# Self attention of a decoder layer: K and Q projected once a batch on 128 rows and spread to row groups through DRAM; the first cross transposes placed in the self attention's ring of banks

## What is computed

```
x = _layernorm(x + self_attention(x))
x = _layernorm(x + cross_attention(ctx_1024, x, mask))
x = _layernorm(x + experts(x))

# self attention, x: [8, 256, 128]
q, k, v = x @ Wq.T, x @ Wk.T, x @ Wv.T         # split into 16 heads of 8
scores = einsum('bhtc,bhkc->bhtk', q, k) * 8 ** -0.5, causal
out = softmax(scores) @ v, heads joined, @ Wo.T
```

## Time and profile before

| | us |
|---|---|
| median of 3 runs | 1153.52 (1153.27 to 1154.64) |
| the profiled execution | 1154.32 |
| its span, from first to last instruction | 1152.5 |
| PE busy | 1104.0 (96%) |
| DVE busy | 879.1 (76%) |
| ACT busy | 735.5 (64%) |
| POOL busy | 539.6 (47%) |
| mean granted clock of TensorE | 0.996 |

### The profile page before, as it was taken

How to read it: one execution, slowest core, us unless ns; L and a number is a source line. 1 busy time by engine, 2 the same in 40 slices (tenths; PEclk the granted TensorE clock), 3 DMA queues, 4 the chain that set the end, 5 groups by cost and what they waited for, 6 DMA issues and landing times. The chain is left out here.

```text
span 1152.5 us, 27526 instructions
## 1 busy us (share of the span) xinstructions
PE 1104.0 (96%) x8781; PEld 946.9 (82%) x8781; DVE 879.1 (76%) x2786; ACT 735.5 (64%) x1754; POOL 539.6 (47%) x892
## 2 busy tenths in 40 slices
PE   6999997999999999999999999999999998999997
PEld 5888875778888887887888888888788887999997
DVE  7999996888878788778787878877878685655554
ACT  6999996667757666666765766666667565322221
POOL 4666665554574355446456445544644432400101
PEclk9999999999999999999999999999999999999999
DMA  2000011000000000000000000000000003000000
GB/s 92 7 7 11 7 44 38 1 11 1 2 1 11 2 1 11 1 1 11 2 1 1 11 2 1 2 1 2 1 2 1 2 1 96 3 10 6 11 6 11
DMA packets 14685, 12.39 MB, mean 11 GB/s; under 512 B 1361, under 2 KB 13649, under 8 KB 14417
## 3 DMA queue, kind: packets, MB, share of 16 engines
q1 hardware_dynamic: 14128, 10.43, 3.0%
q10 hardware_dynamic: 416, 0.20, 0.1%
HBM read 9.57 MB, written 1.05 MB: 9 GB/s over the span
## 5 line engine op out<-in xcount | busy, mean ns | idle before, releaser
L874 POOL TENSOR_TENSOR xk_parts<-k_raw,xk_parts 64x768 fp32r<-64x768 f32 x128 | 236.1, 1845 | 312.7 <-DVE xk_parts L992 310.0
L1016 DVE CUSTOM_DVE_ANT_0 xmasked<-ps,bar 128x768 f32<-128x768 f32 x256 | 244.3, 954 | 4.2 <-issue 0.6
L1128 PE MATMUL ps<-xk_parts,xq_parts 128*128 128x512 f32 (+1 forms) x1024 | 233.2, 350 | 6.9 <-DVE xq_parts L997 3.4
L929 ACT ACTIVATE xprobs<-xmasked,xlow 128x768 f32<-128x768 f32 x256 | 238.0, 930 | 1.4 <-DVE xlow L1016 1.4
L1134 PE MATMUL ps<-ident,xprobs 128*128 128x128 f32 x1536 | 215.0, 276 | 7.1 <-DVE xlow L1016 6.0
L1128 PEld LDWEIGHTS ps<-xk_parts,xq_parts 128*128 128x128 f32 x1024 | 174.4, 189 | 33.3 <-DVE xq_parts L997 3.8
L1134 PEld LDWEIGHTS ps<-ident,xprobs 128*128 128x128 f32 x1536 | 168.9, 140 | 16.7 <-DVE xlow L1016 10.8
L1145 PE MATMUL ps<-xprobs_t,xvals 128*64 128x256 f32 x1536 | 179.9, 383 | 1.1 <-ACT xprobs_t L935 1.1
L1145 PEld LDWEIGHTS ps<-xprobs_t,xvals 128*64 128x64 f32 x1536 | 104.8, 137 | 57.9 <-issue 10.6
L1021 DVE COPY xprobs_t<-ps 128x768 f32<-128x768 f32 x128 | 121.6, 950 | 3.5 <-PE ps L1134 3.5
L909 ACT ACTIVATE k_raw<-ps 128x768 f32<-128x768 f32 x64 | 52.0, 812 | 105.1 <-PE ps L1102 94.3
(11 more groups left out here) (220 smaller groups left out, 2524.8 us busy)
## 6 DMA issues: line engine op xcount, KB each, us to landing
ctx_in<-in_ctx SPq DMA_DIRECT2D x8, 256.0 KB, 3.3
w_rest<-in_L_ffn_w SPq DMA_DIRECT2D x2, 768.0 KB, 6.4
raw_kv<-in_L_xattn_Wkv SPq DMA_DIRECT2D x1, 1024.0 KB, 5.3
out<-state SPq DMA_DIRECT2D x8, 128.0 KB, 2.0
x_in<-in_x SPq DMA_DIRECT2D x7, 128.0 KB, 2.2
raw_q<-in_L_xattn_Wq SPq DMA_DIRECT2D x1, 512.0 KB, 6.1
wout<-in_L_xattn_Wout SPq DMA_DIRECT2D x1, 512.0 KB, 3.9
keep_all<-in_mask_BxS_bk SPq DMA_DIRECT2D x1, 512.0 KB, 4.7
```

The lines of the kernel that those rows point to most:

```text
L874: pool.tensor_tensor(k_parts[dst, i // 2 % 2, h, :], k_raw[src, :], k_parts[src, i // 2 % 2, h, :].bitcast(F32), ALU.subtract).then_inc(k_ ...
L929: nc.scalar.activation(probs[:, i % 4, :], masked[:, i % 4, :], ACT.Exp, scale=-1.0, bias=low[:, i % 4:i % 4 + 1], accum_out=sums[:, pair ...
L1016: dve.tensor_tensor_reduce(masked[:, i % 4, :], slot(slots.place("S", i), KEYS), bar[:, par, :], 1.0, 3e38, ALU.add, ALU.min, low[:, i % 4 ...
L1128: last = nc.tensor.matmul(slot(s, hi - lo, lo), q_parts[:, pair % 2, h, part, t * P:(t + 1) * P], k_parts[:, pair % 2, h, lo:hi], start=pa ...
```

## The change

**K and Q.** Each batch has one step KQ: six matmuls with the plain 128x128 weights project K and Q for all 16 heads into one bank of 512 columns. ACT rounds the bank once (`flat_hi`), DVE takes the remainder once (`flat_lo`). SP writes both to a buffer in DRAM (256 KB each) and reads them back with six transfers into the row groups of `kq_parts` (`k_parts` and `q_parts` are its halves), each to 32 partitions, four of them of 128 KB and two of 256 KB, 1 MB in all. The reads wait for both writes (`kept`); Q_HEAD and S wait for all six reads (`spread`). `kq_parts` has two halves for batches in turn. The weights are transposed 3 times instead of 9.

**V** is one step of six matmuls and one copy. **x_in** has three buffers instead of two, and SP's list has LOAD(1), then SPREAD(0), SPREAD(1), LOAD(2), SPREAD(2), LOAD(3) and so on, all behind `first_contexts`.

```diff
@@ decoder_layer
+        m.scratch = nc.dram_tensor("flat", [2, 2, P, 2, S], F32, kind="Internal").ap()
-                a.gpsimd(pool, {last: steps(emit, "N1", 5, 0, 1) + steps(emit, "N2", 5, 9, 1),
-                                B: steps(emit, "Y", 1, 9, 1)})
+                a.gpsimd(pool, {B - 2: steps(emit, "N1", 5, 0, 1) + steps(emit, "N2", 5, 9, 1),
+                                last: steps(emit, "Y", 1, 15, 1)})
...
-                a.vector(dve, {B - 2: steps(emit, "STATS", KT, 0, 2),
-                               last: steps(emit, "NORM1", 2, 4, 1) + steps(emit, "NORMED", KT, 13, 0.5),
-                               B: steps(emit, "BAR", 1, 3, 1) + steps(emit, "Y", 1, 7, 1)})
+                a.vector(dve, {B - 3: steps(emit, "STATS", KT, 4, 2),
+                               B - 2: steps(emit, "NORM1", 2, 5, 1),
+                               last: steps(emit, "NORMED", KT, 2, 0.5) + steps(emit, "Y", 1, 12, 1),
+                               B: steps(emit, "BAR", 1, 3, 1)})
@@ self_attention
     pe_order = Order(B, SH, {
-        "S": (SH, -0.5), "PT": (SH, 4.75), "K": (SG, -3.5), "Q": (SG, -4), "V": (T, -4),
-        "T": (1, -5), "R": (SG, 9.75), "PV": (SG, 9.5), "OUT": (1, 24)})
+        "S": (SH, -0.5), "PT": (SH, 4.75), "KQ": (1, -8.25), "V": (1, -8),
+        "T": (1, -10), "R": (SG, 9.75), "PV": (SG, 9.5), "OUT": (1, 24),
+        "TX": (1, -6.5), "TC": (1, -6.25)}, only=FIRST_CROSS)
     dve_order = Order(B, SH, {
-        "S": (SH, -0.5), "K": (SG, -3.5), "Q": (SG, -4.25), "PT": (SH // 2, 5.5),
-        "XLO": (1, -5.25), "RECIP": (SG, 5.75), "NORM": (SG, 10), "OUT": (1, 23.5),
-        "V": (T, -4.5)})
+        "S": (SH, -0.5), "KQ": (1, -7.75), "PT": (SH // 2, 5.5),
+        "XLO": (1, -9.25), "RECIP": (SG, 5.75), "NORM": (SG, 10), "OUT": (1, 23.5),
+        "V": (1, -7.25)})
     act_order = Order(B, SH, {
-        "EXP": (SH, 3), "PT": (SH // 2, 6.75), "K": (SG, -1.75), "Q": (SG, -3), "R": (SG, 11.25),
-        "T": (1, -3.5)})
+        "EXP": (SH, 3), "PT": (SH // 2, 6.75), "R": (SG, 11.25), "KQ": (1, -6), "T": (1, -8),
+        "TX": (1, -4), "TC": (1, -3.75)}, only=FIRST_CROSS)
...
+        def emit(kind, b, par, i):
+            if kind == "LOAD" and b > 0:
+                wait(sp, added, b - 2)
+                wait(sp, loaded_x, 16 * b)
+                sp.dma_start(x_in[:, b % 3, :, :], x_rows[b]).then_inc(loaded_x, 16)
+            if kind == "SPREAD":
+                wait(sp, spread, 96 * b)
+                for n, (flat, done) in enumerate(((flat_hi, flat_hi_done), (flat_lo, flat_ready))):
+                    sp.wait_ge(done, b + 1)
+                    sp.dma_start(m.scratch[par, n], flat[:, :, :].bitcast(F32)).then_inc(kept, 16)
+                wait(sp, full["S"], (b - 1) * SH)
+                sp.wait_ge(kept, 32 * (b + 1))
+                for r, to, part in ((0, slice(0, 2), 0), (1, slice(0, 1), 1), (1, slice(1, 2), 0),
+                                    (2, slice(0, 1), 0), (2, slice(1, 2), 1), (3, slice(0, 2), 1)):
+                    sp.dma_start(kq_parts[32 * r:32 * r + 32, par, to, :, :].bitcast(F32),
+                                 m.scratch[par, part, :, to, :].rearrange("(g p) n c -> p n g c", g=SG)
+                                 ).then_inc(spread, 16)
+        emit("LOAD", 1, 1, 0)
+        for b in range(B):
+            emit("SPREAD", b, b % 2, 0)
+            if 1 <= b < B - 1:
+                emit("LOAD", b + 1, 0, 0)
...
             if kind == "Q_HEAD":
                 g = i // HG
-                pool.wait_ge(q_ready, b * SG + g + 1)
+                pool.wait_ge(spread, 96 * (b + 1))
...
+            if kind == "KQ":
+                act.wait_ge(full["KQ"], b + 1)
+                wait(act, kept, 32 * b)
+                nc.scalar.activation(flat_hi[:, :, :].rearrange("p n s -> p (n s)"), bank(banks.place("KQ", 0)),
+                                     ACT.Copy).then_inc(flat_hi_done, 1)
...
+            if kind == "KQ":
+                dve.wait_ge(flat_hi_done, b + 1)
+                dve.tensor_tensor(flat_lo[:, :, :].rearrange("p n s -> p (n s)"), bank(banks.place("KQ", 0)),
+                                  flat_hi[:, :, :].rearrange("p n s -> p (n s)").bitcast(F32), ALU.subtract
+                                  ).then_inc(flat_ready, 1)
...
+            if kind == "KQ":
+                for n, w in enumerate((1, 0)):
+                    o, wh, wl = bank(s, S, n * S), w_hi[:, w, :], w_lo[:, w, :]
+                    nc.tensor.matmul(o, wh, xt_hi[:, par, :], start=True, stop=False)
+                    nc.tensor.matmul(o, wh, xt_lo[:, par, :], start=False, stop=False)
+                    last = nc.tensor.matmul(o, wl, xt_hi[:, par, :], start=False, stop=True)
+                last.then_inc(full["KQ"], 1)
...
             if kind == "S":
-                pe.wait_ge(k_ready, b * SG + i // HG + 1)
+                pe.wait_ge(spread, 96 * (b + 1))
                 pe.wait_ge(q_head_ready, b * SH + i + 1)
```

More of the change, by code:

```diff
@@ L46, with __init__ @@
 class Order:
-    def __init__(self, batches, units, starts, beyond=()):
-        self.batches, self.beyond = batches, beyond
+    def __init__(self, batches, units, starts, beyond=(), only=(), without=()):
+        self.batches, self.beyond, self.only, self.without = batches, beyond, only, without
         due = []
@@ L65, in has @@
     def has(self, kind, batch):
-        return 0 <= batch < self.batches + (kind in self.beyond)
+        if kind in self.only:
+            return batch == self.batches
+        return 0 <= batch < self.batches + (kind in self.beyond) and (kind, batch) not in self.without
     def run(self, emit, between=None, done=(), left=()):
@@ L338, in self_attention @@
     xt_lo = sb(mem, "xt_lo", [P, 2, S], F32R)
-    round_kq = sb(mem, "round_kq", [P, 2, S], F32R)
-    k_parts = sb(mem, "k_parts", [P, SG, S], F32R)
-    q_parts = sb(mem, "q_parts", [P, 2, S], F32R)
+    flat_hi, flat_lo = (sb(mem, "flat_" + n, [P, 2, S], F32R) for n in ("hi", "lo"))
+    kq_parts = sb(mem, "kq_parts", [P, 2, 2, SG, S], F32R)
+    k_parts, q_parts = (kq_parts[:, :, n, :, :] for n in range(2))
     q_head = sb(mem, "q_head", [P, 4, S], F32R)
@@ L362, in self_attention @@
     weights = sem("a_weights")
-    full = {k: sem(f"a_{k}_full") for k in ("T", "K", "Q", "V", "S", "PT", "R", "OUT")}
+    full = {k: sem(f"a_{k}_full") for k in ("T", "KQ", "V", "S", "PT", "R", "OUT")}
     xh_done, x_ready = sem("a_xh_done"), sem("a_x_ready")
-    kh_done, k_ready = sem("a_kh_done"), sem("a_k_ready")
-    qh_done, q_ready = sem("a_qh_done"), sem("a_q_ready")
+    flat_hi_done, flat_ready = sem("a_flat_hi_done"), sem("a_flat_ready")
+    kept, spread = sem("a_kept"), sem("a_spread")
     q_head_ready = sem("a_q_head_ready")
@@ L417, in sync @@
         first_contexts()
-        def load(kind, b, par, i):
-            if isinstance(b, int) and b == 0:
-                return
-            wait(sp, added, b - 1)
-            wait(sp, loaded_x, 16 * b)
-            sp.dma_start(x_in[:, par, :, :], x_rows[b]).then_inc(loaded_x, 16)
-        Order(B, SH, {"LOAD": (1, -SH)}).run(load)
+        def emit(kind, b, par, i):
[20 more added lines that the diff above has]
+                emit("LOAD", b + 1, 0, 0)
         sp.dma_start(wout[:, :, :], m.xwout.rearrange("(r p) d -> p r d", p=P)).then_inc(loaded_rest, 16)
@@ L469, in gpsimd, with scalar @@
         pool_order.run(emit, between)
-    def scalar(act, between=None):
+    def scalar(act, cross, between=None):
         act.dma_start(x_in[:, 0, :, :], x_rows[0]).then_inc(loaded_x, 16)
@@ L521, in vector @@
         dve.memset(vals[:, :, :, :, :], 0.0)
-        link(dve.memset(part[:, :], 0.0))
-        for rows, col in ((slice(32, 64), 0), (slice(96, 128), 0), (slice(64, 96), 1), (slice(96, 128), 1)):
-            last = dve.memset(part[rows, col:col + 1], -1.0)
-        link(last)
         dve.wait_ge(consts, 5)
@@ L618, in emit @@
                 for j in range(T):
[L619 removed]
+                    last = nc.tensor.transpose(bank(s, P, j * P), x_in[:, b % 3, j, :], ident[:, :])
                 last.then_inc(full["T"], 1)
[L621 to L622 removed]
+            if kind in ("KQ", "V"):
+                pe.wait_ge(weights, 2)
                 pe.wait_ge(x_ready, b + 1)
[L624 to L629 removed]
@@ L630, in emit @@
-            if kind == "V":
-                wh, wl = wv_hi[:, :], wv_lo[:, :]
-                xh, xl = (a[:, par, i * P:(i + 1) * P] for a in (xt_hi, xt_lo))
-                nc.tensor.matmul(bank(s, D), xh, wh, start=True, stop=False)
-                nc.tensor.matmul(bank(s, D), xh, wl, start=False, stop=False)
-                nc.tensor.matmul(bank(s, D), xl, wh, start=False, stop=True).then_inc(full["V"], 1)
+            if kind == "KQ":
[5 more added lines that the diff above has]
+                last.then_inc(full["KQ"], 1)
@@ new lines, in emit @@
+            if kind == "V":
+                wh, wl = w_hi[:, 2, :], w_lo[:, 2, :]
```

(7 more changed lines are left out.)

119 lines of the change are left out of this document (48 added, 71 removed).

## The result

The changed kernel takes 1207.66 us (median; 1206.47 to 1208.38), beside 1153.47 us for the kernel before: a ratio of 1.0467, 95% interval [1.0448, 1.0485]. It is slower by 54 us, where I had forecast +8.3 and a range up to 1174. The sign is right, the size is far off.

The account below looks back on a forecast made before the run. ACT was taken to set the pace, with a DRAM wait added to its loop. Start +7.7, seven passages +3.8, last batch -2.0 and step to cross attention -1.2 gave +8.3 us: 1162 us forecast, range 1155 to 1170, eight in ten 1147 to 1174.

Parts of the forecast that it names:

- the second loop: From ACT's T over xt_lo, KQ, V and OUT to R(0): stall 2.6 us, floor 21.4 us a batch.
- the step to the cross attention: Passing from self to cross attention: -1.2 us, between 0 and -2, including cross Q(0) starting 0.8 sooner.
- Term 2: Seven passages from one batch to the next at 22.0 instead of 21.46 us: +3.8, from 0 to about +17.
- flat_lo at 1.4: DVE's remainder of K and Q is ready 1.4 us after ACT's KQ starts, as in the setup.
- The six reads at 5.3: SP's reads from DRAM, 1 MB together, take 5.3 us; ends 4.3 to 5.8.
- the half rate: Rival: reads onto 32 rows run at half rate and take 7.5 us; total about 1179; chance 0.13.
- S(0) to R(2) at 3.9: From PE's S(0) to ACT's R(2) in a batch: 3.9 us, putting R(2) at 14.0 after KQ.
- clock: Rival: PE's clock falls in each stall, costing 1 to 1.5 us a batch; total 1169 to 1173; chance 0.15.
- the DRAM wait: ACT stalls 3.2 us between KQ and R(2), 14.0 against 10.8 of own work; batch 18.8 + 3.2 = 22.0.
- Term 1: Start: first exponential at 23.1 instead of 15.40 us, +7.7; ends +6.3 and +9.5.
- Term 3: Last batch, without spread: fewer roundings, added y evacuations, POOL's 1.19 wait moved away; -2.0 us, from -3.5 to +1.
- The faster rival: Stalls do not arise and ACT's work decides: 19.3 us a batch, total 1143; chance 0.17.

Follow-up runs that it names:

- e1: Changed kernel with OUT's addition placed behind KQ in DVE's list: 1197.13 us.
- e3: Changed kernel with the six reads each going to all 128 partitions instead of 32, so the scores are not the reference's: 1195.52 us.
- g1: Changed kernel with the edits of e1 and e3 and the cross-preparation places of f2: 1181.84 us.
- e4: Changed kernel with only the first two batches spread through DRAM, later batches using their data again: 1182.61 us.
- e2: Changed kernel with 48 filler transposes on PE before S(0) of batches 1 to 7: 1204.26 us.
- e6: Changed kernel with SP's two context loads behind the first spread instead of ahead of it: 1204.94 us.
- f2: Changed kernel with three cross-preparation places moved: statistics earlier on DVE, N2 later on POOL, y_lo behind POOL's last q_head: 1203.90 us.

## Why the prediction was wrong in size

**What held.** ACT's work a batch fell as worked out. Both loops through the fixed lists exist (e1, e3 and g1 for the one, e4 for the other): R(2) to the next KQ took 8.06 us, which was the 22.0 - 14.0 of the sum, and the second loop's floor was 21.9 against 21.4. At the step to the cross attention the first Q no longer waits for the addition: it starts at 247.37, 0.28 before the addition at 247.65, where it came 0.48 behind it, which is the 0.8 forecast. That all behind the eighth addition is 1.1 us shorter (-1.2 forecast) proves less: the executions of the kernel before differ by 2.4 us among themselves. The write took 2.4 us from flat_lo's end to the reads' issue (2.6 forecast with its semaphore).

**Term 2, the seven passages: +3.8 forecast, +39.3 measured.** The step that failed is the time from ACT's KQ to its R(2), 14.0 forecast and 19.2 measured. By the parts of the steady loop:
- flat_lo at 1.4 after KQ: it came at 3.05. I took the pair of the setup, where DVE is free, and did not ask what stands ahead of KQ in DVE's list. It is OUT's addition, which waits for PE (+1.65; e1).
- The six reads at 5.3, 5.4 with their semaphore: 7.7 to the first q_head (+2.3; e3 gives back 1.25 of it by its rows and the order of its pieces). About 0.5 is the issues, 3.25 us for six and not 0.46 each; what the remainder is stays open. The rows I had were all onto 128 partitions. I had named the half rate as a rival with 0.13.
- S(0) to R(2) at 3.9: 5.3 (+1.4). All of it is TensorE at the lower clock behind a stall of 4.3 us: at 1.00 the stretch takes 3.7 (e1) or 3.6 (e2). The 3.9 was right for the upper level. This was a rival with 0.15.

The sum was near its own threshold: the DRAM wait I forecast exceeded the second loop's by only 0.6 us, so every further microsecond on that way counted in full, seven times. The rivals were priced as alternatives, while nothing kept them apart: half rate (+17) and clock (+7 to +11) happened together (the slower reads by +2.3 a passage, near the rival's 2.2, the clock by about 1.6), on top of a term that I had not seen. My ends for this stall were 1.7 to about 5 us; by the same measure (ACT's work of 10.8 taken off) it was 8.4. For a DVE that comes late I had allowed 0.5, without looking at what it would be late by.

**Term 1, the start: +7.7 forecast, +10.1 measured.** The same six reads, 7.5 instead of 5.4 from issue to q_head. That the contexts hold SP up was right, and e6 shows 3.5 us for it.

**Term 3, the last batch: -2.0 forecast, +3.65 measured.** I had POOL's chain move to a batch where the DRAM wait covers it. It did: f2 takes its waits out of the batches with a spread, and they are not shorter. But the change puts y_lo into the last batch, ahead of two q_heads, and I left out this wait of 2.95 us, longer than the 1.19 that went:

```profile
231.38 1.80 POOL L890 TENSOR_TENSOR y_lo<-y,y_hi 128x768 fp32r<-128x768 f32 x1 [2.95 <-DVE y_hi L999]
```

TensorE's clock was 0.93 on average in that passage, 1.00 before. With y_lo behind the q_heads f2 gets 2.7 of the 3.65 back.

**The faster rival** (19.3 us a batch once ACT's work decides) was not this kernel, but it was not far: five and a half places in three lists make it 20.49, and the way through DRAM then costs only the start.

## What to carry to other kernels

A detour through DRAM costs its full length unless its first step stands earlier in every list it passes through; write the loop once round, from an engine back to itself, with what stands ahead of each step in each list, and compare it with the work in between. Once such a loop is exposed, price its uncertain terms together and times the number of batches, not as rivals that exclude each other. A step moved between engines' lists needs each engine's lead over the others: a place that is right on one engine can be some heads too early on another, and another wait may hide that until it is gone.
